# Layer norms of a four-layer graph network: statistics instruction per tile and one scaled difference, in place of five passes over the chunk

## What is computed

```python
x = _layernorm(x + L0(...))   # GCN: degree-normalized sum over edges
x = _layernorm(x + L1(...))   # gated graph network, 2 rounds: message sum, GRU cell
x = _layernorm(x + L2(...))   # graph attention; ends in a layer norm of its own, with gamma and beta
x = _layernorm(x + L3(...))   # message passing; ends in a layer norm of its own, with gain and bias

def _layernorm(x, axis=-1, eps=1e-05):
    m = jnp.mean(x, axis=axis, keepdims=True)
    v = jnp.var(x, axis=axis, keepdims=True)
    return (x - m) / jnp.sqrt(v + eps)
```

## Time and profile before

| | us |
|---|---|
| Median of 3 runs (lowest, highest) | 10851.04 (10847.27, 10852.4) |
| The profiled execution's own time | 10841.94 |
| Its span, first to last instruction | 10840.2 |
| VectorE busy in the span | 5239.4 |
| POOL busy in the span | 4873.9 |
| TensorE busy in the span | 6085.7 |
| Mean granted TensorE clock | 0.729 |

### The profile page before, as it was taken

How to read it: one execution, slowest core, us unless ns; L and a number is a source line. 1 busy time by engine, 2 the same in 40 slices (tenths; PEclk the granted TensorE clock), 3 DMA queues, 4 the chain that set the end, 5 groups by cost and what they waited for, 6 DMA issues and landing times. The chain is left out here.

```text
span 10840.2 us, 166167 instructions
## 1 busy us (share of the span) xinstructions
PE 6085.7 (56%) x60710; PEld 5246.5 (48%) x60711; DVE 5239.4 (48%) x7210; ACT 1520.1 (14%) x4256; POOL 4873.9 (45%) x5701
## 2 busy tenths in 40 slices
PE   4666669996433343443333333586999635545554
PEld 3333349995233333323333333485999624444444
DVE  7888878885211111121222222697888643323333
ACT  3666640001100000000000000132000001111111
POOL 2121200001477777757777777001000147777775
PEclk7777779998766666666666666555999867777777
DMA  1000032222222122221111111475222112222222
GB/s 46 0 0 0 0 51 83 83 83 98 91 66 66 53 66 66 66 71 53 53 52 52 52 52 52 170 292 189 101 93 93 57 53 79 79 80 77 74 79 73
DMA packets 322858, 798.38 MB, mean 74 GB/s; under 512 B 157570, under 2 KB 196012, under 8 KB 303436
## 3 DMA queue, kind: packets, MB, share of 16 engines
q1 hardware_dynamic: 147804, 423.30, 11.6%
q0 software_dynamic: 153216, 312.49, 10.2%
q10 hardware_dynamic: 21744, 61.34, 1.4%
HBM read 714.98 MB, written 81.79 MB: 74 GB/s over the span
## 5 line engine op out<-in xcount | busy, mean ns | idle before, releaser
L984 POOL DMA_INDIRECT ggnn_edges_G<-trans_d,ggnn_edges_rid x3136 | 2975.3, 949 | 1230.9 <-issue 955.1
L1097 PE MATMUL ggnn_edges_PS<-ggnn_edges_OH,ggnn_edges_G 128*128 128x128 f32 x6272 | 1178.2, 373 | 2317.4 <-DMA ggnn_edges_G<-trans_d,ggnn_edges_rid 2207.3
L1097 PEld LDWEIGHTS ggnn_edges_PS<-ggnn_edges_OH,ggnn_edges_G 128*128 128x128 f32 x6272 | 1138.2, 285 | 2362.0 <-issue 2359.0
L984 POOL DMA_INDIRECT mpnn_edges_G<-msg_d,mpnn_edges_rid x1568 | 1500.1, 957 | 689.0 <-issue 473.1
L1053 DVE TENSOR_TENSOR acc<-acc,ggnn_edges_PS 128x128 f32 x224 | 64.4, 288 | 2512.0 <-PE ggnn_edges_PS L1097 2512.0
L1081 PE MATMUL mpnn_edges_PS<-wt_late,mpnn_edges_at 128*128 128x256 f32 x1568 | 543.3, 519 | 684.8 <-DVE mpnn_edges_G L1040 341.9
L620 ACT ACTIVATE prep_OJF<-prep_OJ,prep_fld 128x98 bf16<-128x98 bf16 x3136 | 848.9, 362 | 554.5 <-DVE prep_OJ L676 554.5
L1081 PEld LDWEIGHTS mpnn_edges_PS<-wt_late,mpnn_edges_at 128*128 128x128 f32 x1568 | 413.5, 271 | 796.6 <-DVE mpnn_edges_G L1040 363.0
L826 PE MATMUL prep_PS<-prep_OJF,prep_OHr 128*128 128x490 bf16 x1582 | 583.9, 552 | 214.7 <-DVE prep_OHr L705 214.7
L1040 DVE TENSOR_TENSOR mpnn_edges_G<-mpnn_edges_G,mpnn_edges_PS 128x1792 f32<-128x1792 f32 x112 | 226.2, 2020 | 883.6 <-DMA mpnn_edges_G<-msg_d,mpnn_edges_rid 708.6
L1018 DVE SCALAR_TENSOR_TENSOR ggnn_edges_OH<-dstI,ggnn_edges_itm,ggnn_edges_PS 128x896 f32<-128x896 f32 x448 | 491.5, 1144 | 229.4 <-issue 164.6
(11 more groups left out here) (454 smaller groups left out, 10937.2 us busy)
## 6 DMA issues: line engine op xcount, KB each, us to landing
ba_rows<-slot_d SPq DMA_DIRECT2D x49, 3136.0 KB, 11.4
HB<-slot_d SPq DMA_DIRECT2D x49, 1568.0 KB
heads_rows<-slot_d SPq DMA_DIRECT2D x49, 1568.0 KB
ggnn_edges_G<-trans_d,ggnn_edges_rid POOLq DMA_INDIRECT x3136, 2.5
mpnn_edges_at<-in_edge_attr SPq DMA_DIRECT2D x112, 448.0 KB, 4.5
trans_d<-gcn_edges_tb ACTq DMA_DIRECT2D x49, 512.0 KB, 2.7
trans_d<-ggnn_edges_tb ACTq DMA_DIRECT2D x49, 512.0 KB, 2.9
mpnn_edges_G<-msg_d,mpnn_edges_rid POOLq DMA_INDIRECT x1568, 2.5
```

Of the source, the lines that this page charges most:

```text
L984: pool.indirect_dma_start(G[:, s, c, :], None, table, bass.IndirectOffsetOnAxis(ap=rid[:, s, c:c + 1].bitcast(U32), axis=0)).then_inc(gath ...
L1097: mm = pe.matmul(wp[s % 2], G[:, s, c, :], OH[:, s % 2, c, :], start=c == 0, stop=c == GC - 1)
```

## The change

In `norm`, the mean and the variance come from `bn_stats` on each of the 7 tiles (6 values per row and tile, into the front of `sq`) and `bn_aggr` on each of these (mean and variance, right behind them in `sq`). One instruction adds epsilon. After root and reciprocal, each tile gets one `tensor_scalar` that subtracts the mean and multiplies by the reciprocal root, both read as one value per partition. Only the last instruction of each group of seven is followed by a wait; `norm` has 4 such steps where it had 7.

```diff
--- before.py
+++ after.py
@@ -310,18 +310,25 @@
 
         def norm(dve, own, r, sq, st, var_ready, rooted, turn, n, k):
 
-            r3, q3 = r.rearrange("p (t f) -> p t f", f=D), sq.rearrange("p (t f) -> p t f", f=D)
-            own.step(V.tensor_reduce(st[:, 0:TC], r3, AX, ALU.add))
-            own.step(V.tensor_scalar(st[:, 0:TC], st[:, 0:TC], 1.0 / D, None, ALU.mult))
-            own.step(V.tensor_tensor(out=r3, in0=r3, in1=over(st[:, 0:TC], D), op=ALU.subtract))
-            own.step(V.tensor_tensor(out=q3, in0=r3, in1=r3, op=ALU.mult))
-            own.step(V.tensor_reduce(st[:, TC:2 * TC], q3, AX, ALU.add))
-            V.tensor_scalar(st[:, TC:2 * TC], st[:, TC:2 * TC], 1.0 / D, EPS, ALU.mult, ALU.add).then_inc(var_ready, 1)
+            r3 = r.rearrange("p (t f) -> p t f", f=D)
+            parts = sq[:, 0:TC * 6].rearrange("p (t k) -> p t k", k=6)
+            whole_ = sq[:, TC * 6:TC * 8].rearrange("p (t k) -> p t k", k=2)
+            for t in range(TC):
+                ins = V.bn_stats(parts[:, t, :], r3[:, t, :])
+            own.step(ins)
+            passed(dve, tick)
+            for t in range(TC):
+                ins = V.bn_aggr(whole_[:, t, :], parts[:, t, :])
+            own.step(ins)
+            V.tensor_scalar(st[:, TC:2 * TC], whole_[:, :, 1], EPS, None, ALU.add).then_inc(var_ready, 1)
             dve.wait_ge(rooted, turn * n + (k + 1))
             own.step(V.reciprocal(st[:, TC:2 * TC], st[:, TC:2 * TC]))
-            own.step(V.tensor_tensor(out=r3, in0=r3, in1=over(st[:, TC:2 * TC], D), op=ALU.mult))
-
-        NORM_STEPS = 7
+            for t in range(TC):
+                ins = V.tensor_scalar(r3[:, t, :], r3[:, t, :], whole_[:, t, 0:1], st[:, TC + t:TC + t + 1],
+                                      ALU.subtract, ALU.mult)
+            own.step(ins)
+
+        NORM_STEPS = 4
 
         def root(act, st, var_ready, rooted, turn, n, k):
             act.wait_ge(var_ready, turn * n + (k + 1))
```

## The result

The changed kernel takes 10798.54 us (median of 5 runs, 10792.75 to 10805.47), against 10851.04 before (5 runs). The ratio is 0.9954 [0.9943, 0.9966]: 52.5 us, or 0.46%, faster. The forecast was 10801 us. The profiled execution took 10792.75 us.

The account below looks back on a forecast made before the run. No engine fills the span; what counts is the 18 norms at which VectorE's work ends last. Terms 36.7 + 2.4 + 5.0 + 6.2 = 50.3 us, taken from 10851.0, gave 10801 us, range 10785 to 10832.

Parts of the forecast that it names:

- What bounds the kernel: 18 of 42 norms fully on the path (14 in gat); the other 24, beside ScalarE or POOL, matter only by delays.
- The norm: Each norm on the path falls from 6.51 to 4.47 us, saving 2.04; 18 of them give 36.7 us.
- Statistics: In each norm, seven statistics instructions, 0.28 us long and 0.20 apart, take 1.52 us.
- Aggregation: In each norm, seven aggregations of 6 values, 0.17 us long and 0.09 apart, take 0.75 us.
- Epsilon, root and reciprocal: In each norm, this part stays as before, 0.68 us.
- scaled difference: In each norm, seven instructions of 0.28 us, 0.20 apart, subtract and multiply in 1.52 us.
- gcn: Chunks 1 to 6: ScalarE's wait before its root goes, then the table's DMA limits; 0.4 us each, 2.4 in all.
- mpnn's slots: At two of seven mpnn chunk ends POOL no longer waits for a row number; 2 x 2.5 = 5.0 us.
- POOL's long gathers: ggnn and mpnn gathers lengthened beside VectorE's two-tensor passes, 12.4 us in all, get shorter; 6.2 us taken as the middle.
- Two cycles per element: Rival: statistics take twice as long per element, 0.93 us more per norm; 31 us saved, 10820 us; chance 0.11.
- Full price: Rival: the new small instructions don't overlap, a norm takes 5.9 us; 20 us saved, 10831 us; chance 0.09.
- The reciprocal's rate: Rival: statistics run at the reciprocal's rate, 4.7 us more per norm; 73 us slower, 10924 us; chance 0.06.

Follow-up runs that it names:

- gat_only: The changed kernel with the new norm in gat alone (14 of 42 norms), the old one elsewhere: 12593.3 us, ratio 0.9998 to the kernel before.
- second profile: The full change run once more on another chip, against the kernel before: 10806.01 us, ratio 0.9955.
- wait_each: The full change plus a semaphore wait after each statistic and each scaled difference: 12561.96 us, ratio 0.9989 to the kernel before; run again, 12552.07 us, 0.9991.
- pool_again: The new norm in ggnn and mpnn alone (21 of 42 norms), the old one elsewhere: 10831.64 us, ratio 0.998 to the kernel before.
- direct: The full change, with the last norm of a chunk in gcn, gat and mpnn writing straight into `X`, without the copy: 12487.09 us, 0.9933 of the kernel before.
- direct_third: Another run of the full change with last norms in gcn, gat and mpnn written straight into `X`: 12483.37 us, ratio 0.9932 to the kernel before.

## Why the prediction was right, and where its terms were off

- **What bounds the kernel.** Right. The norms that were called covered still run, and cost nothing but what they do to POOL; the 14 of gat show in full (`gat_only`).
- **The norm, 4.47 us forecast, 4.81 measured.** Statistics 1.60 against 1.52: length and step as taken from the lower bound, and 0.15 of gap behind them in place of 0.04. A separate semaphore increment (`passed`) stands in that gap; behind the differences there is 0.03 without one (before line 1662) and 0.15 with one (before the copy into `X`). Aggregation 0.61 against 0.75: 0.149 long, 0.07 apart. Epsilon, root and reciprocal 0.69 against 0.68.
- **The term that was mis-sized is the scaled difference, 1.91 against 1.52.** I had "an operand read per partition adds 53" and added it once, but the instruction reads two. 227 + 2 x 53 = 333, and 340 was measured. Line 285 of the same kernel is a `tensor_scalar` on 128 x 128 floats with one such operand, and takes 287 ns: 227, 287 and 340 with none, one and two. The 0.08 of overlap held, so the step grew with the length. With the smaller errors of the other parts a norm gains 0.34 less, 18 x 0.34 = 6 us on the path, and 4.8 of the 5.9 us that gat fell short.
- **gcn.** The succession (root no longer waits, DMA of the table late next) is right; I took the middle of 0 to 0.82. The bound came from one chunk and does not hold (1.25 in the third of the six); the mean over the six is 0.66, 1.5 us more gain in all.
- **mpnn's slots.** 5.0 forecast, 4.5 found. One idle time of 0.86 us (before the gather at 9750.76) is left, where I had expected none over 0.3.
- **POOL's long gathers.** 6.2 forecast, "the middle"; 6.1 + 2.4, 8.4 unrounded, found. The middle was no mechanism. By the instruction that runs when a gather starts, the norm's own passes cost 12.4 us before, and its instructions cost 0.85 now: gathers never come out longer beside the statistics, and lose at most 0.08 beside the differences. But the next gather now meets what follows: 2.3 us are lost anew with the copy into `X`, and the rest of the 4 us that did not go with the passes around the norm. Gathers over 1 us became fewer, as forecast, 58 in place of 69 in the two stages.
- **The sum.** With measured terms: 18 x 1.70 = 30.6, 6 x 0.66 = 3.9, 4.5 and 8.4, together 47 us; forecast 50.3, measured 52.5 by the medians and 49.2 by the spans (36.1 in the second profile, 47.9 by its medians). The agreement within 3 us is partly luck: 6 us too much on the norms, against 3 to 4 too little on gcn and POOL, and scatter of 5 to 10 us in the long stretches.
- **Rivals.** Two cycles per element: out, a statistic of 128 elements is 0.276 long, as a plain pass is. Full price: out, by the step of 0.196, and `wait_each` shows what it would have looked like, even dearer in gat than I had put it (1.6 us per norm, where I had 1.4). The reciprocal's rate: out.

## What to carry to other kernels

Many small instructions can beat few long passes, but only with the waits between independent neighbours left out: with them the norm would have taken 6.38 us in place of 6.51. Price a new instruction from the nearest row of the same shape and count each operand it reads per partition separately. An engine that matters only by holding others up shows its gain in their rows: look for instructions that are longer than their median, and at what was already running on the other engine when they began.

## What was not expected

**Chips differ.** On three of the chips the kernel before takes 12.56 to 12.60 ms. The long stages ggnn and mpnn carry nearly all of that (4988.4 and 2667.6 us in `gat_only`, where 3985 to 3990 and 1971 to 1982 are usual: 1684 of 1740 us), while gat and gcn are unchanged. There TensorE is late: matmuls of line 1119 that belong together (line 1104 of the changed kernel) come one per 2.8 us in places. `gat_only`'s timeline of TensorE:

```profile
6032.64 0.37 PE L1119 MATMUL ggnn_edges_PS<-ggnn_edges_OH,ggnn_edges_G 128*128 128x128 f32 x1 [2.42 <-issue]
6035.44 0.37 PE L1119 MATMUL ggnn_edges_PS<-ggnn_edges_OH,ggnn_edges_G 128*128 128x128 f32 x1 [2.43 <-issue]
6038.24 0.37 PE L1119 MATMUL ggnn_edges_PS<-ggnn_edges_OH,ggnn_edges_G 128*128 128x128 f32 x1 [2.43 <-issue]
```

Idle time before that line's matmuls and weight loads with nothing to wait for (us, times), in `gat_only`:

```profile
  issue: 6650.0, 3292
```

In `pool_again`, on a chip of the first kind, the same row:

```profile
  issue: 2720.2, 244
```

3292 idle stretches in place of 244 that nothing in the profile explains. TensorE's granted clock is lower there as well (0.68 over the span against 0.73; 0.50 in the stretch shown, the 1.2 GHz level), but that is not where the time is: a matmul of this line in ggnn takes 342 ns in the mean, against 373 in `pool_again`, and the gaps around it take the rest. The gap is before the engine issues and follows no wait, so the supply of instructions may be the cause; that is a guess, no run tests it, and it stays open. With TensorE that late, POOL no longer runs without a pause: in `gat_only` it waits 77 times in ggnn for row numbers. A change made for POOL's sake is then worth something else, and which engine bounds a stage depends on the chip. `direct` and `direct_third` were 88 and 81 us under the kernel before on these chips, against 63 on the first kind; gat accounts for the same 27 to 28 us on both, and where the rest comes from is not shown.
